# A top-k mask moved from ScalarE to GpSimd in a two-layer decoder kernel, with a new order of work

## The reference, cut to what matters

```
scores = einsum('bhqd,bhkd->bhqk', Q, K) / sqrt(16)          # 256 x 256 for each of 16 heads
vals, idx = top_k(scores, 25)                                # 25 of the 256 keys of each row
sparse = zeros.at[rows, idx].set(vals)                       # the other 231 hold 0, not minus infinity
attn = softmax(sparse)
out = (attn @ V) @ Wo + bo
```

## Time and profile before

| | us |
|---|---|
| median of three runs | 6784.98 |
| lowest and highest | 6783.06, 6803.64 |
| profiled execution, its own time | 6756.82 |
| its span | 6755.0 |
| PE busy (matmuls) | 5896.7, 87% |
| DVE busy | 4510.2, 67% |
| ACT busy | 4012.6, 59% |
| POOL busy | 1507.3, 22% |
| granted PE clock, mean | 0.899 |

### The profile page before, as it was taken

The page is one execution under the profiler, slowest core; times in us unless marked ns, Lnnn a source line. Parts: engine busy times, 40 slices in busy tenths (PEclk is TensorE's granted clock), DMA queues, the critical chain, the costliest instruction groups (busy, mean ns, idle before and its releaser), DMA issues. The chain is left out here.

```text
span 6755.0 us, 109667 instructions
## 1 busy us (share of the span) xinstructions
PE 5896.7 (87%) x37509; PEld 3877.2 (57%) x37762; DVE 4510.2 (67%) x16186; ACT 4012.6 (59%) x9761; POOL 1507.3 (22%) x2564
## 2 busy tenths in 40 slices
PE   6888988988988988898888898888898898898876
PEld 3565565565565565565565565566556556556542
DVE  1366766666777666776676676666776666677653
ACT  2465666565666665666656566656566655566632
...
PEclk7789989899999899999999899999998999999965
...
GB/s 79 4 6 6 4 8 6 8 8 6 4 8 7 6 8 6 4 8 8 6 8 6 6 6 8 6 8 7 7 4 8 6 8 8 6 4 8 4 2 5
DMA packets 29456, 54.18 MB, mean 8 GB/s; under 512 B 8145, under 2 KB 9810, under 8 KB 27986
## 3 DMA queue, kind: packets, MB, share of 16 engines
...
...
## 5 line engine op out<-in xcount | busy, mean ns | idle before, releaser
L914 POOL TENSOR_TENSOR t_pr<-t_pr,sc 128x512 f32<-128x512 f32 x512 | 649.6, 1269 | 1495.9 <-ACT t_pr L839 1495.9
L350 DVE TENSOR_REDUCE m_nm<-bankM 128x2 f32<-128x512 f32 x1024 | 657.0, 683 | 347.9 <-PE bankM L340 344.0
L887 DVE MATCH_REPLACE8 wk<-m,wk 128x256 f32<-128x256 f32 x2048 | 821.0, 408 | 0.0
L340 PE MATMUL bankM<-m_kT,m_q 32*128 32x256 f32 x4096 | 698.5, 466 | 75.4 <-DVE m_nm L350 74.3
L883 DVE MAX8 m<-wk 128x8 f32<-128x256 f32 x2048 | 759.2, 412 | 0.0
L651 ACT ACTIVATE xk_area<-bankH,xb 64x256 f32<-64x256 f32 x1024 | 480.7, 469 | 460.4 <-PE bankH L546 438.1
L394 PE MATMUL bankM<-m_q,m_kT 32*128 32x512 f32 x2048 | 627.9, 691 | 0.0
L883 DVE MAX8 m<-sc 128x8 f32<-128x256 f32 x1024 | 380.0, 412 | 327.5 <-ACT sc L830 290.1
L340 PEld LDWEIGHTS bankM<-m_kT,m_q 32*128 32x128 f32 x4096 | 411.3, 216 | 312.4 <-DVE m_nm L350 133.6
L845 ACT ACTIVATE t_pr<-t_pr,t_nm 128x256 f32<-128x256 f32 x1024 | 463.9, 504 | 182.5 <-POOL t_pr L914 180.5
L408 ACT ACTIVATE m_pT<-bankM,keymask 128x512 f32<-128x512 f32 x512 | 323.7, 683 | 247.4 <-PE bankM L394 247.4
...
## 6 DMA issues: line engine op xcount, KB each, us to landing
...
```

Source lines behind the costliest of these rows:

```text
L340: last = nc.tensor.matmul(bank[x][:, j * S:(j + 1) * S], b["q2"][r:r + 32, e, j, t * P:(t + 1) * P], b["kT"][r:r + 32, e, :], start=not ma ...
L350: nc.vector.tensor_reduce(b["nm"][:, i % 2, 2 * (i // 2) + x, :], banks[u % 3][:].rearrange("p (j s) -> p j s", j=2), AX.X, ALU.max, negat ...
L887: m = nc.vector.match_replace(out=wk[:, k, t, :], in_to_replace=take, in_values=src[:, t, :], imm_value=-BIG)
L914: nc.gpsimd.tensor_tensor(sp_[:, u % 2], taken[:, u % 2], sc[:, u % 3], ALU.mult).then_inc(g["sp_mul"], 1)
```

## The change

ScalarE no longer makes the mask. GpSimd makes it from `wk` with one comparison (is -BIG: 1, else 0), between the row maximum and its copy, one head at a time, 16 in a pass. The condition for writing into `t_pr` (transposes of head u-2 done) goes with it, from ACT's queue into POOL's. The four order strings are new throughout.

```diff
@@ ORDER: all four strings new; the first line of "act" as an example @@
-        t h c m h4 c2 t h3 t7 h4 t h t h3 c h2 t h t h2 t h c h t3 h3 t h3 t h t h t2 h3 t h4 t3 h4 t h t h4 t h t2 h c3 h2 t c2 h3 t c2 t2
+        t h c m h4 c3 t h3 c t7 h2 t2 h2 t h6 t h2 t2 h6 t h3 c3 t h c2 h4 c2 h3 c2 t h3 c2 h2 t2 c3 t3 h c2 t h3 c2 t h2 c t2 h t3 c t h4 t
...
@@ scalar_t @@
             for u in range(H):
                 yield
-                act.wait_ge(g["sp_top"], u + 1)
-                if u >= 2:
-                    act.wait_ge(g["spa_tr"], u - 1)
-                nc.scalar.activation(taken[:, u % 2].rearrange("p t s -> p (t s)"), wk[:, u % 2].rearrange("p t s -> p (t s)"),
-                                     ACT.Relu, bias=-1.0, scale=-2.0 / BIG).then_inc(g["sp_tk"], 1)
-                yield
                 act.wait_ge(g["sp_mul"], u + 1)
@@ pool_t @@
                 nc.gpsimd.tensor_scalar(mx0[:, u, :], m8[:, u % 2, 0, :, 0], 0.0, -1.0, ALU.max, ALU.mult).then_inc(g["sp_nm"], 1)
+                yield
+                if u >= 2:
+                    pool.wait_ge(g["spa_tr"], u - 1)
+                nc.gpsimd.tensor_scalar(taken[:, u % 2], wk[:, u % 2], -BIG, 1.0, ALU.is_equal, ALU.mult).then_inc(g["sp_tk"], 1)
                 yield
                 pool.wait_ge(g["sp_nm"], u + 1)
```

More of the change, by code:

```diff
@@ L60 @@
     "pe": runs("""
[L61 to L62 removed]
+        t h c m h2 c2 t h2 c t c t c h c t h c t h2 c h3 c h t c h2 c h3 c t c3 h c2 h2 c2 t h c2 h t c t c3 t h c2 t c t h c h t h c t c t2
+        h3 t c2 h2 t h m t m2 t m t m h2 m h t m t h t m h2 m t h m h2 m h m t m t m2 t m2 h t m2 h m2 t m t h m2 h2 m h8 t m h m t m t m t
+        m t m t"""),
     "act": runs("""
[L64 to L66 removed]
+        t h c m h4 c3 t h3 c t7 h2 t2 h2 t h6 t h2 t2 h6 t h3 c3 t h c2 h4 c2 h3 c2 t h3 c2 h2 t2 c3 t3 h c2 t h3 c2 t h2 c t2 h t3 c t h4 t
+        h t h t3 h c h4 t h t m t m3 h m t2 h2 t2 h2 t h5 t h t h t h t h t h t h2 t m t m2 t m2 t2 m2 h t2 m2 t h m2 h t m2 t m h3 t m2 h
+        t2 m2 t m t m t"""),
     "dve": runs("""
[L68 to L69 removed]
+        t h c m c t c t h2 t c2 h c2 t c4 t2 c2 t2 c2 t2 c2 t c2 t2 c2 t7 h7 t9 c3 t h t2 c t c t c t c h2 t m t m t c m t3 h2 t3 m2 t m2 h
+        t h2 t m2 h t m2 t m2 t m2 t m2 t m2 t4 h t h t h t h t4 h8 t h t4 h m3 t3 m t"""),
     "pool": runs("""
[L71 removed]
+        t h c m c t c t2 h3 t8 c t8 h3 t12 c3 h t4 m2 t4 h t4 h3 t8 m t4 h3 t12"""),
 }
```

7 lines of the change are left out of this document (removed).

## The result

The changed kernel takes 6868.6 us (median of 4 runs, 6851.4 to 6882.9) against 6784.0 for the one before: ratio 1.0127, 95% interval 1.0089 to 1.0165. It is slower, where 6741 us and faster were forecast. The time lies inside the range (6580 to 6890) and on the wrong side of no change.

A forecast was written before the change was run, and what follows sets the result against it. No engine is full; PE is nearest (87% busy), losing time to waits and a lowered clock. Terms sum to -1.5 us a pass, -44 us over 29 passes: 6741 us median, range 6580 to 6890.

The forecast's parts named there:

- A: Transposed scores of stage m: other work fills PE's waits, idle 3.8 to 1.0 us, -2.8 us a pass (-3.3 to 0).
- B: Scores of stage c, moved between projections: idle 2.5 to 0.5 us, -2.0 us a pass (-2.5 to 0).
- rival 3: Idle time only changes its place; gain inside +-0.7 us a pass, 6785 us; chance 0.13.
- C: Scores of stage m: clock falls there and partly comes back, 25.7 to 29 us, +3.3 us a pass.
- rival 1: Clock stays up in the scores of stage m: -2.7 there, -7.5 us a pass in sum, 6567 us; chance 0.20.
- D: Output and layernorm chain of stage c: 0 us a pass, bounds -2 to +2.
- layernorm hits: Layernorm halves slowed on DVE by POOL's 128x512 additions: at most 0.9 us each, one or two hits 1 to 2 us.
- E: Barrier and the short clock fall (0.95) in stage c's transposed scores: same pieces, 0 us.
- The mask: Comparison on POOL taken as 0.8 us each, 13 us a pass (3.5 to 20); POOL stays far from full.
- that sign of being wrong: Prediction is wrong if L907 waits for PE's transposes and L300 or L571 wait behind it.
- The sum: -2.8 - 2.0 + 3.3 = -1.5 us a pass, over 29 passes -44 us.
- Rival 2: Low clock holds through all the scores of stage m: +4.0 us a pass, +116, 6901 us; chance 0.22.

The follow-up runs named there:

- a2: Kernel before, old order, with only the mask moved from ScalarE to GpSimd: 6788.1 us, ratio 1.0012 to the kernel before.
- a4: Changed kernel plus twelve unused matmuls a pass, six ahead of each of the first two steps of stage c's transposed scores: 6581.1 us, ratio 0.9697.
- a8: Changed kernel plus the twelve unused matmuls of a4, and the mask computed for one column in each row tile: 6605.5 us, ratio 0.9751.
- a6: Changed kernel plus six unused matmuls a pass, ahead of the first step of stage c's transposed scores only: 6742.1 us, ratio 0.9958.
- b5: Kernel before, with stage c's copy m_m made three times in sequence, so the first step of its transposed scores waits: 6792.1 us, ratio 1.0046.
- d1: Changed kernel with transpose L437 moved from ahead of the first step of stage c's transposed scores to behind its values: 6893.9 us, ratio 1.0179.
- a5: Changed kernel with the mask computed for one column in each row tile, the rest left out: 6737.5 us, ratio 0.9912; two more executions took 6852 and 6899.

## Why the prediction was wrong

Lengths and idle times of a place are those of one pass; low times are means of 28.

- **A, transposed scores of stage m, -2.8.** Right as to this place: 25.0 - 24.1 = 0.9 us idle, where 1.0 was kept.
- **B, scores of stage c, -2.0.** Right as to this place: 28.5 - 28.3 = 0.2 us idle, where 0.5 was kept. But the gain of A and B did not reach the pass. In the same pass the idle time of the transposed scores of stage c went from 2.9 to 5.1 us and that of the scores of stage m from 2.2 to 4.6, and over the loop it stayed (21.3 and 21.5 us a pass). That is rival 3's mechanism, the idle time that only changes its place, which had 0.13.
- **C, scores of stage m, +3.3.** Wrong in sign. The place takes 23.1 us at a clock of 0.93: rival 1's 23, not 29. Low time 128 to 160 us behind the move went from 14.4 to 7.3 us, worth -3.6 us a pass. The long low stretch did not stay here, though what the prediction gave as its cause, score matmuls on few rows with waits between, did.
- **D, output and layernorm chain, 0.** Off by its bound: the clock is 0.89 in the pass shown, and low time 104 to 128 us behind the move went from 1.7 to 5.8 us: +2.0, the upper bound. The layernorm hits that the bound was made for did not come here: the one new hit stands some 9 us behind the move, and those of stage h went.
- **E, "same pieces, 0".** The step that failed. The transposed scores of stage c keep their pieces but not what stands between them and ahead of them. The old order has L589 and then 1.35 us of waiting, and a fall of 3 to 4 us in most passes; the new one has 1.72 and 1.35 us of waiting and low stretches of 17 to 48 us. Low time here went from 6.7 to 27.1 us, (27.1 - 6.7) / 2 = +10.2 us a pass. The sum had no term for m_m, which now stands behind six copies on ACT (128.1 us of waiting in the whole execution, 11.7 before). I had weighed the clock only in the place where it was low before, and taken the mean of 0.95 for a place that was safe, when it was one already close to falling.
- **The mask, 0.8 us and a cost of 0.** The duration was wrong, 1.94 us, and outside both bounds: a two-input product of the same shape was no upper bound for it (1.27 us). By the Trainium skill's GPSIMD Engine Reference, section Performance pitfalls for Q7 kernels, the estimate was 0.44 to 0.87 us; the trace does not agree (1.94 us). That it costs hardly anything was right (a2: 1.0012; a4 against a8: some 1 us a pass), as POOL is busy only 36% of the span. L907 never waited for PE's transposes in the changed kernel, so that sign of being wrong did not come. That its load doesn't slow the top-k was right too (412 ns in a2).
- **The sum.** The clock takes 8.6 us a pass: +10.2 (E), +2.0 (D), -3.6 (C). At the full clock the new order gains 3.6, where rival 1 had it at 7.5, so even without the fall in E the sum was 3.9 too hopeful. Rival 2 named nearly the size (6901) and a pass of 205 us (205.9 measured), but by luck: it had the low clock in C, and it sat in E. That the time lies inside the range is luck too, since no bound of the range allowed for E.

**What stays open.** Why the clock stays low so long in the new order. With the second wait of 1.35 us alone it is 17 us there (a6) and 3 to 4 in most passes of the kernel before; with two waits 17 to 48 there and 7 or 10 in the old order (b5). The place of L437 is not it (d1). That the time at the low level differs from pass to pass, and in a5 from run to run, with the same instructions, suggests that small shifts of time decide it; no run tests that.
